# Key-token sums and attention weights in fp32, and a channel mask ahead of the box additions, in a fused four-layer image kernel

## The reference

```
x = x + L0(gn(x))   mixture of 8 pointwise convolutions, gates by sparsemax of the pooled input
x = x + L1(gn(x))   3x3 depthwise conv, bn, relu, prune; 1x1 conv, bn, relu, prune
x = x + L2(gn(x))   attention over the 784 pixels, with squared and normalised q and k
x = x + L3(gn(x))   3x3 mean filter (the box)
```

## Time and profile before

| | before |
|---|---|
| median of three runs | 1683.83 us |
| the profiled execution | 1683.19 us, its span 1681.4 us |
| TensorE busy | 1543.4 us (92%) |
| VectorE busy | 1452.5 us (86%) |
| ScalarE busy | 1369.0 us (81%) |
| GpSimd busy | 421.4 us (25%) |
| mean granted clock of TensorE | 0.972, and 1.00 from 200 to 1500 us |
| DMA | 33 GB/s over the span |

### The profile page before, as it was taken

How to read it: one execution, slowest core, us unless ns; L and a number is a source line. 1 busy time by engine, 2 the same in 40 slices (tenths; PEclk the granted TensorE clock), 3 DMA queues, 4 the chain that set the end, 5 groups by cost and what they waited for, 6 DMA issues and landing times. The chain is left out here.

```text
span 1681.4 us, 26750 instructions
## 1 busy us (share of the span) xinstructions
PE 1543.4 (92%) x8190; PEld 1144.9 (68%) x8190; DVE 1452.5 (86%) x2530; ACT 1369.0 (81%) x3496; POOL 421.4 (25%) x269
## 2 busy tenths in 40 slices
PE   3569999999999999999999999999999999998994
PEld 2247777677777767777776777777677777766773
DVE  5867799999989999998999999899999989998646
ACT  3368988888888888888888888888888888878872
POOL 1111212233321223332122333212233321223224
PEclk8689999999999999999999999999999999999997
DMA  4000011100111110011111001111100111000000
GB/s 143 20 20 20 20 39 39 39 20 20 39 38 38 38 38 19 19 38 38 38 38 38 19 19 38 38 38 38 38 19 19 38 38 39 20 20 20 20 20 39
DMA packets 21058, 55.58 MB, mean 33 GB/s; under 512 B 2321, under 2 KB 3345, under 8 KB 21010
## 3 DMA queue, kind: packets, MB, share of 16 engines
q1 hardware_dynamic: 20914, 54.98, 9.3%
q10 hardware_dynamic: 96, 0.00, 0.0%
HBM read 29.29 MB, written 25.69 MB: 33 GB/s over the span
## 5 line engine op out<-in xcount | busy, mean ns | idle before, releaser
L769 DVE SCALAR_TENSOR_TENSOR h<-xpad,dw_sb,h 128x784 f32<-128x784 f32 x512 | 534.3, 1097 | 1.1
L540 PE MATMUL tile_ps<-wqk,xn_parts 128*112 128x512 f32 x1344 | 363.6, 425 | 0.0
L540 PEld LDWEIGHTS tile_ps<-wqk,xn_parts 128*112 128x112 f32 x1344 | 234.6, 175 | 80.2
L1223 POOL TENSOR_SCALAR xpad<-x,gn_r,gn_s 128x784 f32<-128x784 f32 x64 | 64.8, 1020 | 784.1 <-DVE gn_s L700 784.1
L448 PE MATMUL conv_ps<-h,pw_masked 128*128 128x392 f32 x512 | 183.5, 502 | 42.6 <-DVE x L805 37.1
L582 PE MATMUL tile_ps<-k,xT 112*128 112x256 f32 x896 | 205.1, 388 | 7.7 <-ACT xT L1029 7.7
L582 PEld LDWEIGHTS tile_ps<-k,xT 112*128 112x128 f32 x896 | 174.2, 195 | 40.1 <-issue 8.4
L963 ACT ACTIVATE junk<-x 128x784 bf16<-128x784 f32 x192 | 163.1, 851 | 40.6 <-DVE x L805 20.7
L570 PE MATMUL conv_ps<-x,mixed 128*128 128x392 f32 (+1 forms) x512 | 177.4, 499 | 2.2 <-ACT mixed L997 1.1
L448 PEld LDWEIGHTS conv_ps<-h,pw_masked 128*128 128x128 f32 x512 | 93.4, 192 | 111.6 <-DVE x L805 38.7
L448 PE MATMUL conv_ps<-xn_parts,w_out 128*128 128x392 f32 x768 | 153.1, 348 | 0.0
(11 more groups left out here) (143 smaller groups left out, 3020.5 us busy)
## 6 DMA issues: line engine op xcount, KB each, us to landing
x<-x SPq DMA_DIRECT2D x32, 784.0 KB, 4.3
out<-x SPq DMA_DIRECT2D x32, 784.0 KB, 3.5
expert_sb<-expert_rows SPq DMA_DIRECT2D x8, 256.0 KB, 5.5
x<-w_qk SPq DMA_DIRECT2D x1, 512.0 KB
x<-w_vT SPq DMA_DIRECT2D x1, 256.0 KB
x<-w_ln SPq DMA_DIRECT2D x1, 256.0 KB
pw_sb<-pw_wT SPq DMA_DIRECT2D x1, 256.0 KB
gmean<-group_mean SPq DMA_DIRECT2D x1, 64.0 KB, 4.0
```

Source lines behind the costliest of these rows:

```text
L540: mm = nc.tensor.matmul(bank, xn2_parts[:, u, i, m * TOK:(m + 1) * TOK], wqk[:, v, i, :], start=False, stop=(i == J - 1 and u == 1))
L769: ins = nc.vector.scalar_tensor_tensor(acc, view, scalar, acc, ALU.mult, ALU.add)
```

## The change

kx is copied out of PSUM once, as fp32, by ScalarE; VectorE's low part of it is gone, with its semaphore. The combined output weights are kept in fp32 too (a new tile, filled in the setup, from which the split parts for the other user are made). In `attention_weights` two fp32 products per half take the place of six split ones. On VectorE `h_mask` stands in front of `box_sums` instead of behind it.

```diff
-        kx_parts = sb("kx_parts", [P, 2, J, C], F32R)
+        kx = sb("kx", [P, J, C])
+        w_out_full = sb("w_out_full", [P, J, C])
...
-        kx_hi = sig("kx_hi")
-        kx_lo = sig("kx_lo")
+        kx_read = sig("kx_read")
...
             def attention_weights(E):
 
-                pe.wait_ge(kx_lo.sem, kx_lo.at(E))
+                pe.wait_ge(kx_read.sem, kx_read.at(E))
                 pe.wait_ge(ksum_read.sem, ksum_read.at(E))
                 for c in range(J):
                     dst = tile_ps[:, ATTN_BANK, c * C:(c + 1) * C]
                     nc.tensor.matmul(dst, k_rows[:, 0, half(c)], bv_ln[:], start=True, stop=False)
                     for i in range(J):
-                        for u, v in ((0, 0), (0, 1), (1, 0)):
-                            mm = nc.tensor.matmul(dst, kx_parts[:, u, i, half(c)], w_out[:, v, i, :], start=False,
-                                                  stop=(i == J - 1 and u == 1))
+                        mm = nc.tensor.matmul(dst, kx[:, i, half(c)], w_out_full[:, i, :], start=False, stop=(i == J - 1))
                 mm.then_inc(attn_w_mm.sem, 1)
...
                 dve.wait_ge(setup_pe, 2)
-                parts_of(w_out, tile_ps[:, 0, :].rearrange("p (i c) -> p i c", i=J))
+                did(nc.vector.tensor_copy(w_out_full[:], tile_ps[:, 0, :].rearrange("p (i c) -> p i c", i=J)))
+                parts_of(w_out, w_out_full[:])
...
-            def kx_low(E):
-                dve.wait_ge(kx_hi.sem, kx_hi.at(E))
-                nc.vector.tensor_tensor(kx_parts[:, 1], tile_ps[:, KX_BANK, :].rearrange("p (i c) -> p i c", i=J),
-                                        kx_parts[:, 0].bitcast(F32), ALU.subtract).then_inc(kx_lo.sem, 1)
-
             def step(t):
                 Z, A, B, C_, D, E, F = (t + 1 - n for n in range(STAGES))
                 if A.started:
                     variances(A)
                     scales_shifts(A)
-                if E.active:
-                    kx_low(E)
                 if A.active:
                     gate_logits(A)
...
                 if B.active:
                     depthwise(B, slice(1, 3))
+                if C_.active:
+                    h_mask(C_)
                 if F.active:
                     box_sums(F, range(BOX_STEPS))
-                if C_.active:
-                    h_mask(C_)
                 if B.active:
                     depthwise(B, slice(3, 5))
...
-            def kx_high(E):
+            def kx_copy(E):
                 act.wait_ge(kx_mm.sem, kx_mm.at(E))
                 if (E - 1).active:
                     act.wait_ge(attn_w_mm.sem, attn_w_mm.at(E - 1))
-                nc.scalar.copy(kx_parts[:, 0], tile_ps[:, KX_BANK, :].rearrange("p (i c) -> p i c", i=J)
-                               ).then_inc(kx_hi.sem, 1)
+                nc.scalar.copy(kx[:], tile_ps[:, KX_BANK, :].rearrange("p (i c) -> p i c", i=J)
+                               ).then_inc(kx_read.sem, 1)
...
-SETUP_DVE = SETUP_BN + 10 + 2 + 2 + 2
+SETUP_DVE = SETUP_BN + 10 + 2 + 1 + 2 + 2
```

More of the change, by code:

```diff
@@ L1141, in step @@
                 if E.active:
-                    kx_high(E)
+                    kx_copy(E)
                 if E.active:
```

## The result

| | before | after |
|---|---|---|
| median, measured side by side (4 runs each) | 1683.65 us | **1695.53 us** (1694.24 to 1697.62) |
| ratio, 95% interval | | 1.0072 (1.0054 to 1.0089) |
| the profiled execution | 1683.19 us | 1696.47 us |
| its span | 1681.4 us | 1694.7 us |
| mean granted clock | 0.972 | 0.974 |

The change makes the kernel 0.7% slower. The profiled execution came out at 1696.47 us, and its span grew by 13.3 us. In the groups of the experiments further down, three or four of 17 runs of the kernel before lie some 5 us under the others (1678 to 1680 us, granted clock 0.976 against 0.972), which may be why a ratio there and the two medians can differ by about 1 us.

A forecast was written before the change was run, and what follows sets the result against it. A loop of waits between VectorE and TensorE was taken as the bound; 27 x (0.05 + 0.36) = 11.1, pipeline end 0.9, products without a wait 1.0 and setup 0.4 made +13.4: 1696.6 us, range 1685.5 to 1702.5.

The forecast's parts named there:

- The loop: VectorE from gate logits to first x3 half (18.8 us), TensorE from pointwise products to next logits (30.3): turn 49.1 us.
- Part 1: TensorE in attention_weights: four fp32 products replace twelve split ones; block 2.64 us, +0.05 us per image on the path.
- Part 2: VectorE ahead of the logits: without kx_low 0.69 us less per image, worth 0, as the wait at L720 grows.
- Part 3a: Input of VectorE's moved mask: 0.7 us slack, no new wait in 27 images; 0.9 us in sum at the end.
- the late step: Step near the end where ScalarE is later: VectorE stands 2.4 us for the mask's input, x3 0.7 us later.
- the four products: attention_weights blocks with no wait in front, first image with weights and last three: 4 x 0.25 = 1.0 us.
- Part 3c: GpSimd's two mask multiplications fall beside VectorE's third and fourth box additions: 0.14 + 0.22 = 0.36 us per image.
- No price for the new place: Rival: GpSimd's multiplications slip through without holding VectorE; +3.7 us, 1686.9 us; chance 0.20.
- A lost turn: Rival: GpSimd's fourth box addition goes ahead of VectorE's first, 0.52 us per image; +17.7 us, 1700.9 us; chance 0.13.
- The whole of both: Rival: VectorE stands for all of both GpSimd multiplications; +29.0 us, 1712.2 us; chance 0.03.
- TensorE gains: Rival in attention_weights: fp32 products at 0.38 us, multiplications free for VectorE, 0.19 us saved per image; 1679.6 us; chance 0.10.
- the setup: Once, before the first image's x1: one more VectorE copy out of PSUM, next cast reading SBUF; net +0.4 us.

The follow-up runs named there:

- the mask alone: The kernel before with only the channel mask moved in front of VectorE's box additions; 1691.07 us, ratio 1.0045.
- the products alone: The changed kernel with the channel mask back behind VectorE's box additions (fp32 products, no kx_low, setup copy stay); 1687.63 us, ratio 1.0025.
- GpSimd's wait: The changed kernel, but GpSimd waits for VectorE's last box addition before multiplying the weights by the mask; 1692.14 us, ratio 1.0050.

## Why the prediction was right

**The loop** held. The turn grew from 49.09 to 49.46 us, by 0.37 where 0.41 was forecast, and by its two stretches: VectorE's +0.31, TensorE's +0.06.

**Part 1** held. The block takes 2.61 us (2.64 forecast), its start no longer waits, and TensorE's stretch grew by 0.06 (0.05). The 0.44 us per fp32 product of `keys_x` was the right row for it.

**Part 2** held in what it says of the time and was wrong about the place. VectorE lost 21 us of work and the end came no sooner for it. But the wait at the logits did not grow to over 1 us per image, as the prediction named for a sign; it stayed at 16.4 us in all, and the wait at L844 grew, from 16.9 to 48.2 us. VectorE waits at two points ahead of the logits, and the first that it comes to took the time up. The view of the waits of before lists that one too, at 16.9 us beside the 16.4 of L720, and the prediction read only the second.

**Part 3a** held: no new wait in the full images (14.7 us in 5 pieces, from 8.6 in 3, all near the end). In the late step VectorE stood 2.31 us for the mask's input, where 2.4 was read:

```profile
1539.96 1.31 DVE L776 TENSOR_SCALAR hmask<-h_over 128x2 f32<-128x2 f32 x1 [2.31 <-ACT over L1067]
```

x3 of that step came 1.4 us later against its turn, not 0.7. And TensorE, which waited 2.42 us for it instead of 1.22, went on at a lower granted clock (0.60 instead of 1.00), so that its eight products took 4.57 us instead of 2.87, a cost that the prediction didn't have. In the kernel before, the clock was lower a little later (0.78) and the products of `keys_x` in the same step took 7.97 us, where they now take 6.28, so this evens out. But in the last step `keys_x` took 9.20 us before (clock 0.67) and 7.97 after (0.78), and that gave 1.2 us back. From the last logits to the end it is 210.32 us instead of 209.44, +0.88, where 0.9 and three of the four products (0.75) were forecast; without the 1.2 us of the last step it is 2.1.

**Part 3c** is the term that decided, and it was a little too large: two instructions grew by 0.16 us each, 0.31 in the stretch, where 0.14 + 0.22 = 0.36 was taken from the earlier trace rows. The row chosen, taps beside the same multiplications, was near enough: the mask alone gives the same 0.31; doubling the multiplications then gave 0.22 for each tap. The masked weights are ready 3.7 us ahead of the products instead of 0.3, and that was worth nothing, as said.

The rule of the Trainium skill, page "SBUF — State Buffer", section "SBUF: two separate sides", that the engine which starts first holds the port pair for its whole instruction, would have made 0.94 us of this. The runs show 0.14 to 0.22 us for each instruction of VectorE that meets a multiplication, so the price of 0.94 is out. Whether a multiplication holds the ports for less than its 0.47 us, or part of the hold falls where VectorE doesn't need them, the trace doesn't show. For the mask, held 1.84 us behind an addition of GpSimd, it agrees.

**The rivals.** *No price for the new place*: out, both the kernel after and the one with the mask alone show 1.13 to 1.14. *A lost turn*: out, VectorE's first addition started at 851.99, ahead of GpSimd's fourth at 852.13, for the reason given. *The whole of both*: out. *TensorE gains*: out, the products alone are slower by 0.25%.

**The sizes.** By stages of the two traces, the sum of 13.3 us splits thus:

| | forecast | measured |
|---|---|---|
| turns of the full loop | 27 x 0.41 = 11.1 | 26 turns, 9.75 |
| from the start to the sixth image's logits | 0.4 + 0.25 | 2.65 |
| from the last logits to the end | 0.9 + 0.75 | 0.88 |

The sum of 13.4 was met partly because errors cancel, and that is luck. The loop was counted with one turn too many and at 0.41 instead of 0.37. The end was 0.77 too high, thanks to the clock in the last step. The start was too small by 2.0: the setup took 0.51 (0.4 forecast), and the next three turns took 1.02, 0.80 and 0.32 us more.

The 1.02 of the first of these turns, to the fourth image's logits, lie in 16 pointwise products, before and after:

```profile
77.85 7.30 PE L448 MATMUL conv_ps<-h,pw_masked 128*128 128x392 f32 x16 [5.50 <-issue]
...
78.35 8.34 PE L448 MATMUL conv_ps<-h,pw_masked 128*128 128x392 f32 x16 [5.49 <-issue]
```

The granted clock over them is 0.75 before and 0.66 after. With the mask alone they take 8.05 us at 0.68, with the products alone 8.23 at 0.66, with GpSimd's wait 8.20 at 0.67. The rest of the turn is the same within 0.05 us, but that with GpSimd's wait the products begin 0.9 us sooner, since GpSimd's first multiplication took 1.09 us there instead of 1.95, and so this turn is as short as before. In the next turn 0.5 of the 0.80 are the clock again (the first six products of queries and keys, 1.79 us before, 2.29 after), and 0.30 is the block in `attention_weights`, with no wait in front of it, which was forecast at 0.25. The 0.32 of the third is that block once more. So 1.5 of the 2.0 us come from TensorE staying at its lower level somewhat longer in the start of this execution, which is no part of the mechanism. Why it did, and whether it does so in each execution, is open: there is one trace of each kernel.

The experiments agree in size: 3.2 to 4.2 us for the products (26 x 0.05 = 1.3, 0.5 for the setup and 0.25 to 0.30 for each of five blocks without a wait make 3.1 to 3.3) and 6.7 to 7.6 for the mask (26 x 0.31 = 8.1). The clock in the start and the end moves more than what is left.

## What to carry to other kernels

Before costing an edit, find the stretches that close the loop from wait to wait, here 18.8 us of VectorE and 30.2 of TensorE. Work removed ahead of a wait is worth nothing until other work is moved into the gap: without `kx_low` the kernel was no faster in the order of the change and 14 us faster once two taps stood ahead of the logits. And with two engines that hold each other up, the place of a small operation decides its price: look for what it runs beside in the new order, and price it by a row in which these two already meet.

## What the runs showed of the hardware

- A multiplication of 128x256 on GpSimd, 0.47 us alone, lengthens an instruction of VectorE with 128x784 elements beside it by 0.14 to 0.22 us. Issued while VectorE's taps follow one another, it is itself held for 1.72 to 1.94 us and costs VectorE nothing, as long as no second one gets in before the taps end. What decides between the two kinds of turn is open.
- An operation of 128x2 elements on VectorE is held as long as a large one behind an addition of GpSimd: it takes 1.84 us where it takes 0.16 alone, and an addition of 128x784 in the same place takes 2.66 where it takes 0.98, 1.68 us more each.
- TensorE's granted clock stayed at 1.00 through pauses of up to 1.73 us in every turn of the changed kernel's full loop, and fell to 0.53 behind pauses of 2.04 to 2.17 us in 20 of 24 turns of the one with doubled multiplications, which cost 1.7 us in the next eight products and 1.2 in the turn.
- Executions of nearly the same kernel differ by where the granted clock is low in the start: 16 products took 7.30 us at 0.75 and 8.34 at 0.66, enough to hide or feign an effect of 1 us.
